# A state-space layer behind attention and experts: the convolution split into even and odd tokens

## Chip, core and metric

One core of one Trainium2 chip runs the whole program. The time is the device time of one execution in microseconds (us). A profile of one further execution gives the rows.

## What is computed

Four layers act on `x` of 8 x 512 tokens by 256 features, in float32, each with a layer norm ahead of it and a residual sum behind it. The third is the one that the change is about:

```
x = x + linear_attention(layernorm(x))        # 16 heads
x = x + one_of_8_experts(layernorm(x))        # 256 -> 512 -> 256, top expert by a router
x = x + ssm(layernorm(x)):
    xc, z = split(x @ in_proj.T)              # 512 and 512 channels
    u  = conv1d(xc, conv_w[512,512,4 taps], causal) + conv_b      # over tokens
    dt = clip(sigmoid(u @ dt_w.T + dt_b), 1e-4, 1);  B, C = u @ B_w.T, u @ C_w.T
    state[t] = exp(clip(dt*A)) * state[t-1] + dt*B*u + 1e-6       # 512 channels x 16 states
    y  = sum over states(state * C) + D*u;  out = (y * silu(z)) @ out_w.T
x = x + one_of_8_experts(layernorm(x))        # the same expert weights again
```

Per output channel the convolution is a sum over 4 taps and 256 features, since the kernel first multiplies the projection and the taps together into one weight `tapw`.

## The kernel before, in words

The program has five parts on one time axis: attention (to some 182 us), a router and the preparation of expert tiles (to 238), 39 expert tiles (to 393), the state-space layer (to 1263), and router and expert tiles once more (to 1469).

The engines are PE (matmul), ACT (activations and copies), DVE (vector), POOL (GpSimd) and SP (issues DMAs). Each runs its own list of instructions in order, and semaphores tie them together.

The state-space layer walks over 8 batches. A batch has 16 states by 4 channel tiles, `SLOTS` = 64 slots. In each slot `g`:

- ACT computes a decay `exp(dt*a)` for slot `g + 3` (`m_decay`, L745) and a quarter of the inputs of the next state (`m_input`, L755).
- PE turns the inputs from tokens-on-partitions to channels-on-partitions with four transposes into one of three banks (`m_spread`, by the helper of L1300).
- DVE runs the recurrence over 512 tokens (`m_scan`, L1197).
- After every four slots POOL multiplies the four results by the row of C (`c_product`, L500) and issues a DMA that adds them to one of two running sums, even or odd states (`add_on`, L509).

Beside the slots of batch `b`, the engines do the preparation of batch `b + 1` (`m_prep` on PE, `m_pre` on ACT and DVE) and the close of batch `b - 1` (`m_close`, `m_late`, `m_skip`). At which slot each of these steps stands is written out by hand in tables of slot numbers: `CONV_AT` for the matmuls of the convolution (L1567), `UT_AT` for the transposes of u (L1575), `BC_AT` (L1584), `DT_AT` (L1598), `DTT_AT` (L1613), `Z_AT` (L1629), `OUT_AT` (L1640), `ADD_AT` for DVE's additions of the two running sums (L1147, L1154), `FINAL_AT` (L1159), `SKIP_AT` for ACT's D*u (L736). `SPIN_AT` are three matmuls without use (L1699). DVE's add of the even sum waits for the last even DMA of the batch before, the semaphore `m_chain0`.

The convolution of one channel tile is 8 matmuls of 512 tokens, 4 taps by 2 halves of the features, summed in one bank; ACT then adds the bias and writes u (`m_uevac`, L699). A float32 matmul stands in the profile as two records, called passes here; a transpose is one record.

Before the first slot stands the preparation of batch 0, with nothing to hide behind: layer norm, 4 x 8 matmuls of the convolution, `dt`, transposes, the first inputs, the turning of batch 1 (`m_turn`). Slots begin at 472.25 us. The weights `tapw` are made by 8 products of `ipw` and `cw` (L1449), four beside the first router, four just before the state-space layer. SP loads `ipw` and `cw` at 203 us, behind the stores of attention's result.

The rows of x lie in a ring of four batches in `x`; SP reloads a batch at state 2. The other half of `x` holds buffers of the scan.

## Time and profile before

| | |
|---|---|
| median of 3 runs | 1475.5 us (1467.76, 1475.5, 1475.68) |
| the profiled execution | 1471.08 us, its span 1469.3 us |
| busy, share of the span | PE 93%, DVE 69%, ACT 64%, POOL 59% |
| granted clock of PE, mean | 0.978 |

The shares are means over five parts with different limits. The busy time of PE is over 93% in every part but attention and the routers, so the shares tell little; the rows by batch, further down, tell more. The two parts with experts (238 to 393 us and 1312 to 1469 us) are not touched.

### The profile page before, as it was taken

What the parts mean: (1) busy time and instruction counts of PE and PEld (TensorE: products, weight loads), DVE (VectorE), ACT (ScalarE), POOL (GpSimd) and SP (SyncE); (2) the same over time, 40 slices, a digit from 0 to 9 for tenths busy, and PEclk for the clock granted to TensorE, in tenths of its full rate; (3) what the DMA queues carried; (4) which work ended last, traced back from release to release, by engine and by line L of the source; (5) the groups of instructions that cost most, each with busy time, mean ns of one, the idle gap of its engine ahead of it and who ended that gap; (6) DMA issues with size and microseconds to landing.
All of it is one profiled execution on the core that took longest, in us unless ns stands there. A gap on an engine that the chain in (4) does not pass through costs nothing.

```text
span 1469.3 us, 22230 instructions
## 1 busy us (share of the span) xinstructions
PE 1366.5 (93%) x7040; PEld 949.6 (65%) x7040; DVE 1011.8 (69%) x1529; ACT 937.7 (64%) x1737; POOL 861.1 (59%) x436
## 2 busy tenths in 40 slices
PE   5899998999998999999999999999999887979997
PEld 2566686999744555565655655655656576569996
...
GB/s 301 85 29 29 19 98 144 211 206 210 153 65 16 118 219 195 179 221 186 201 222 181 205 220 176 218 190 193 223 170 204 230 195 234 79 235 203 208 210 82
DMA packets 108229, 248.39 MB, mean 169 GB/s; under 512 B 19097, under 2 KB 49950, under 8 KB 94048
## 3 DMA queue, kind: packets, MB, share of 16 engines
...
q8 instruction: 55, 0.90, 0.2%
...
## 4 chain that ended last, share of the span: by engine, by line
PE 67%; ACT 16%; DVE 10%; issue 4%; DMA 1%; another core or an unknown queue 1%; SPq 0%; DVEq 0%; ACTq 0%; POOLq 0%; POOL 0%
PE ps L1300 11%; PE ps L1513 9%; PE ps L1504 9%; PE ps L1567 7%; ACT arena L745 7%; PE ps L1598 7%; ACT arena L755 7%; PE ps L1325 4%; PE ps L1640 3%; PE ps L1629 3%; DVE arena L1197 3%; PE ps L1362 2%; PE ps L1584 2%; PE ps L1316 2%; PE ps L1449 1%
## 5 line engine op out<-in xcount | busy, mean ns | idle before, releaser
L500 POOL TENSOR_TENSOR arena<-arena 128x2048 f32<-128x2048 f32 x91 | 425.1, 4684 | 118.6 <-DVE arena L1197 117.4
L1300 PEld LDWEIGHTS ps<-cst,arena 128*128 128x128 f32 x2428 | 295.3, 143 | 280.1 <-issue 187.7
L1197 DVE TENSOR_TENSOR_SCAN arena<-arena,ps 128x512 f32<-128x512 f32 x364 | 431.7, 1209 | 62.3 <-PE ps L1300 58.7
L1300 PE MATMUL ps<-cst,arena 128*128 128x128 f32 x2428 | 365.7, 278 | 51.2 <-ACT arena L755 24.3
L745 ACT ACTIVATE arena<-arena,a_neg 128x512 f32<-128x512 f32 x512 | 365.9, 715 | 43.3 <-DVE arena L1197 29.6
L755 ACT ACTIVATE arena<-arena,m_bt 128x512 f32<-128x512 f32 x512 | 362.9, 709 | 3.8 <-DVE arena L1134 2.2
L1567 PE MATMUL ps<-arena,tapw 128*128 128x512 f32 x512 | 255.1, 600 | 0.7 <-ACT arena L693 0.7
L1197 DVE TENSOR_TENSOR_SCAN x<-arena,ps 128x512 f32<-128x512 f32 x148 | 175.7, 1209 | 21.9 <-PE ps L1300 20.6
L500 POOL TENSOR_TENSOR x<-x,arena 128x2048 f32<-128x2048 f32 x36 | 169.8, 4728 | 14.7 <-DVE x L1197 12.7
L1078 DVE TENSOR_TENSOR arena<-ps,arena 128x256 f32<-128x256 f32 x78 | 33.1, 425 | 205.7 <-PE ps L1513 131.4
L456 POOL DMA_INDIRECT arena<-rows,arena x78 | 75.9, 973 | 158.1 <-DVE arena L1058 134.9
L1504 PEld LDWEIGHTS ps<-arena 128*128 128x128 f32 x1248 | 154.7, 196 | 3.8
L1504 PE MATMUL ps<-arena 128*128 128x128 f32 x1248 | 154.9, 279 | 0.0
L1513 PE MATMUL ps<-arena 128*128 x624 | 147.5, 380 | 3.3 <-ACT arena L644 3.3
L637 ACT ACTIVATE arena<-ps 128x256 f32<-128x256 f32 x78 | 30.0, 385 | 157.8 <-PE ps L1300 156.5
L1598 PE MATMUL ps<-arena,dtw 128*128 128x512 f32 x256 | 128.6, 597 | 0.6 <-ACT arena L699 0.6
L1513 PEld LDWEIGHTS ps<-arena 128*128 128x128 f32 x624 | 112.5, 190 | 16.0 <-issue 3.7
L644 ACT ACTIVATE arena<-ps,b1t 128x128 f32<-128x128 f32 x312 | 89.3, 370 | 43.8 <-issue 29.5
L1567 PEld LDWEIGHTS ps<-arena,tapw 128*128 128x128 f32 x512 | 85.1, 193 | 36.1 <-issue 33.7
L447 POOL TENSOR_TENSOR x<-x,arena 128x1024 f32 (+1 forms) x8 | 18.9, 2358 | 120.0 <-DVE arena L868 114.4
L471 POOL DMA_INDIRECT residual<-arena x39 | 39.4, 1011 | 68.4 <-DVE arena L1085 67.2
L471 POOL DMA_INDIRECT out_x<-arena x39 | 39.3, 1008 | 67.5 <-DVE arena L1085 67.5
...
## 6 DMA issues: line engine op xcount, KB each, us to landing
arena<-arena POOLq DMA_DIRECT2D x52, 1024.0 KB, 8.3
...
arena<-c_rows SPq DMA_DIRECT2D x128, 256.0 KB, 3.7
arena<-x POOLq DMA_DIRECT2D x28, 1024.0 KB, 8.4
x<-arena POOLq DMA_DIRECT2D x24, 1024.0 KB, 8.3
...
```

The lines of the kernel that those rows point to most:

```text
L456: g.indirect_dma_start(out=t_x[j % XB], out_offset=None, in_=xs[r], in_offset=bass.IndirectOffsetOnAxis(ap=idx[:, j:j + 1], axis=0))\
L471: g.indirect_dma_start(out=x_mid if r == 0 else T["out"].rearrange("b s d -> (b s) d"), out_offset=bass.IndirectOffsetOnAxis(ap=idx[:, j:j ...
L500: g.tensor_tensor(h, h, m_c[i % RC].unsqueeze(1).to_broadcast([P, KI, SEQ]), ALU.mult)\
L644: last = a.activation(t_ht[par][:, k, :], ps[4 + par][:, k * P:(k + 1) * P], ACT.Relu, bias=b1t[:, row(e), k:k + 1].rearrange("p a b -> p ...
L745: a.activation(m_a[g % RA], m_dt[b % 2][:, k, :], ACT.Exp, scale=a_neg[:, k, n:n + 1])\
L755: a.activation(m_dbt[i % 2][:, c, :], m_wt[b % 2][:, c, :], ACT.Copy, bias=1e-6, scale=m_bt[b % 2][:, c, n:n + 1]).then_inc(S("m_dbt"), 1)
L1197: v.tensor_tensor_scan(out=h[:, k, :], data0=m_a[g % RA], data1=ps[SCAN_BANK[g % 3]][:, :], initial=0.0, op0=ALU.mult, op1=ALU.add).then_i ...
L1300: return t.transpose(bank, src[:, k * P:(k + 1) * P], ident)
L1504: last = t.matmul(ps[4 + par][:, h * P:(h + 1) * P], t_w1[j % WR][:, k, h * P:(h + 1) * P], t_xt[par][:, k, :], start=(k == 0), stop=(k == ...
L1513: last = t.matmul(ps[6 + par][:, 0:D], t_ht[par][:, k, :], w2[:, row(e), k, :].rearrange("p a h -> p (a h)"), start=(k == 0), stop=(k == K ...
L1567: mm = t.matmul(ps[CONV_BANK[o]][:, :], tapw[:, k, d, o * P:(o + 1) * P], m_xt[n % 2][:, d, k:k + SEQ], start=(i == 0), stop=(i == TAPS * ...
L1598: mm = t.matmul(dt_bank(n, o)[:, :], dtw[:, k, o * P:(o + 1) * P], m_u[n % 2][:, k, :], start=(k == 0), stop=(k == KI - 1))
```

## The change

The convolution is computed in two phases of tokens. For an even token and its odd neighbour the four taps are paired, and three products of half the length take the place of four: (1) the sum of two neighbouring taps times the tokens of one phase, which both outputs use, (2) and (3) single taps times the difference of neighbouring tokens, one for each phase. So a channel tile is 12 matmuls of 256 tokens (one 255) in place of 8 of 512. In batches 1 to 7 this is done for tiles 1, 2 and 3, and tile 0 keeps its 8 matmuls; in batch 0 it is done for all four.

What comes with it: POOL forms the sums of taps once for batch 0 (`sum_first`) and once for all others (`tap_sum`), and two differences of tokens per batch after state 15 (`m_differ`, 128 x 512 elements each, every second token of `m_xt`). ACT moves the shared product with the bias into every second column of u (`m_both`, 256 columns) in place of `m_uevac`; DVE adds the two single-phase products to it (`m_join`, 512 columns, the bank read in alternation from its two halves, the shared product read twice each). The sums and the differences lie in `x`, so the ring of rows shrinks to two places: each batch's rows are loaded for the norm at state 8 and again for the final update at state 2 of the next batch but one, on SP. Two batches of rows for the last router are staged in `tapw`.

All tables of slots are rewritten. The add of the even sum goes from slots (7, 8, 10, 15) to (5, 6, 13, 16), and ACT's third D*u now waits for the first final product. SP loads `ipw` and the first two `cw` at the start of the program; the first product of `tapw` stands between the turns of the first router, and the fourth between its counting matmuls. In the preparation of batch 0 the clips and weights of `dt` stand in another order, two of the four inputs of the first slot are computed by DVE, and the turning of batch 1 begins earlier. Semaphores of the two expert stages are shared, which moves no work.

```diff
+HALF = SEQ // 2
+TURN_OF = ((0, 0), (0, 1), (1, 1), (1, 0))
+PARTS, BOTH_END = 3 * len(TURN_OF), len(TURN_OF) - 1
...
-CONV_AT = ((0, 1, 2, 2, 3, 4, 5, 6), (7, 8, 8, 10, 11, 12, 13, 14), (14, 15, 16, 17, 18, 20, 21, 21), (22, 23, 24, 26, 28, 29, 30, 30))
...
+CONV_AT = ((0, 1, 1, 2, 3, 4, 5, 6), (5, 6, 7, 7, 9, 9, 10, 10, 11, 11, 12, 13), (14, 14, 15, 15, 15, 16, 16, 16, 17, 17, 18, 18), (19, 20, 20, 20, 20, 21, 21, 21, 22, 22, 23, 23))
...
+UC_AT = (8, 10, 17, 21)
...
+ADD_AT = ((5, 6, 13, 16), (11, 12, 15, 17))
+FINAL_AT = (11, 15, 18, 19)
+UPDATE_AT = (31, 52)
+STAT_AT = (33, 37, 62, 63)
+SKIP_AT = (0, 4, 12, 17)
+CLIP_AT = (35, 38, 47, 51)
+WT_AT = (39, 41, 50, 58)
...
+        xd_first = first_h(0)[:, 0:2 * KD * HALF].rearrange("p (s k t) -> p s k t", s=2, k=KD)
+        sum_first = first_h(1).rearrange("p (j k n) -> p j k n", j=2, k=KD)
+        m_xd = x[:, CPB:2 * CPB, :].rearrange("p c d -> p (c d)").rearrange("p (s k t) -> p s k t", s=2, k=KD)
+        tap_sum = x[:, 2 * CPB:4 * CPB, :].rearrange("p c d -> p (c d)").rearrange("p (j k n) -> p j k n", j=2, k=KD)
...
+            def send_tap(k):
+                if k >= 2:
+                    sp.wait_ge(S("tap_mm"), KD * (k - 1))
+                sp.dma_start(cw[k % 2], T["conv"][k].rearrange("(k p) d -> p k d", p=P)).then_inc(S(f"ld_cw{k}"), 16)
+
+            sp.dma_start(ipw, T["ip_x"].rearrange("(k p) d -> p k d", p=P)).then_inc(S("ld_cw0"), 16)
+            send_tap(0)
+            send_tap(1)
...
+                    if n == 2 and b >= 2:
                         sp.wait_ge(S("f1_rows"), 16 * (b - 1))
                         if b > 2:
-                            sp.wait_ge(S("ld_again"), 16 * (b - 2))
-                        sp.dma_start(x[:, kept(new):kept(new) + CPB, :],
-                                     x_mid[new * SEQ:(new + 1) * SEQ].rearrange("(c p) d -> p c d", p=P))\
-                            .then_inc(S("ld_again"), 16)
+                            sp.wait_ge(S("ld_late"), 16 * (b - 2))
+                        sp.dma_start(x[:, 0:CPB, :], x_mid[(b - 1) * SEQ:b * SEQ].rearrange("(c p) d -> p c d", p=P))\
+                            .then_inc(S("ld_late"), 16)
+                    if n == N_LOAD and b < BATCH - 2:
+                        sp.wait_ge(S("m_umm"), conv_done(b + 1, KI - 1))
+                        if b:
+                            sp.wait_ge(S("ld_rows"), 16 * b)
+                        sp.dma_start(x[:, CPB:2 * CPB, :],
+                                     x_mid[(b + 2) * SEQ:(b + 3) * SEQ].rearrange("(c p) d -> p c d", p=P))\
+                            .then_inc(S("ld_rows"), 16)
+                    if n == NS - 2 and b == BATCH - 2:
+                        sp.wait_ge(S("m_umm"), conv_done(BATCH - 1, KI - 1))
+                        sp.wait_ge(S("f1_rows"), 16 * (BATCH - 2))
+                        for k in range(RING, BATCH - 2):
+                            sp.dma_start(staged[k], xs[1][k * SEQ:(k + 1) * SEQ, 0:D].rearrange("(c p) d -> p c d", p=P))\
+                                .then_inc(S("ld_back0"), 16)
+                        sp.wait_ge(S("ld_rows"), 16 * (BATCH - 2))
+                        sp.dma_start(x[:, CPB:2 * CPB, :], x_mid[(BATCH - 1) * SEQ:BATCH * SEQ].rearrange("(c p) d -> p c d", p=P))\
+                            .then_inc(S("ld_rows"), 16)
...
+            def sum_taps(out, j):
+                g.tensor_tensor(out[:, j], tapw[:, TAPS - 1 - 2 * j], tapw[:, TAPS - 2 - 2 * j], ALU.add)\
+                    .then_inc(S("m_zero"), 1)
+
+            g.wait_ge(S("tapw"), 2 * KD)
+            sum_taps(sum_first, 1)
+            g.wait_ge(S("tapw"), TAPS * KD)
+            sum_taps(sum_first, 0)
+
+            def m_differ(n):
+
+                g.wait_ge(S("m_xtc"), KD * (n + 1))
+                for s in range(2):
+                    g.tensor_tensor((m_xd if n else xd_first)[:, s], m_xt[n % 2][:, :, PAD + 1 - 2 * s:PAD + SEQ - 2 * s:2],
+                                    m_xt[n % 2][:, :, PAD:PAD + SEQ - 1:2], ALU.subtract).then_inc(S("m_xd"), 1)
+
+            m_differ(0)
+            g.wait_ge(S("m_stat0"), 2)
+            for j in range(2):
+                sum_taps(tap_sum, j)
+            m_differ(1)
+
...
+                if i % NS == DIFFER_AFTER and i // NS < BATCH - 2:
+                    m_differ(i // NS + 2)
...
-            def m_uevac(n, o):
-                a.wait_ge(S("m_umm"), KI * n + o + 1)
+            def m_uevac(n):
+                a.wait_ge(S("m_umm"), conv_done(n, 0, TAPS * KD - 1))
+                if n >= 2:
+                    a.wait_ge(S("m_y0"), KI * (n - 2) + 1)
+                a.activation(m_u[n % 2][:, 0, :], ps[CONV_BANK[0]][:, :], ACT.Identity, bias=mvec[:, 0, 0:1])\
+                    .then_inc(S("m_u"), 1)
+
+            def m_both(n, o):
+
+                a.wait_ge(S("m_umm"), conv_done(n, o, BOTH_END))
                 if n >= 2:
                     a.wait_ge(S("m_y0"), KI * (n - 2) + o + 1)
-                a.activation(m_u[n % 2][:, o, :], ps[CONV_BANK[o]][:, :], ACT.Identity, bias=mvec[:, 0, o:o + 1])\
-                    .then_inc(S("m_u"), 1)
+                a.activation(m_u[n % 2][:, o, 1::2], both_bank(n)[:, o % 2 * HALF:(o % 2 + 1) * HALF], ACT.Identity,
+                             bias=mvec[:, 0, o:o + 1]).then_inc(S("m_both"), 1)
...
+            def m_join(n, o):
+
+                v.wait_ge(S("m_both"), both_done(n, o))
+                if n and o == 1:
+                    v.wait_ge(S("m_u"), KI * n + 1)
+                v.wait_ge(S("m_umm"), conv_done(n, o))
+                u = m_u[n % 2][:, o, :].rearrange("p (t s) -> p t s", s=2)
+                v.tensor_tensor(u, ps[CONV_BANK[o]][:, :].rearrange("p (s t) -> p t s", s=2),
+                                u[:, :, 1].unsqueeze(2).to_broadcast([P, HALF, 2]), ALU.add).then_inc(S("m_u"), 1)
...
+            for c in range(CPB, NCH // 2):
+                row_stats(c)
+            m_join(0, 0)
+            for c in range(NCH // 2, NCH - 1):
+                row_stats(c)
+            link(row_stats(NCH - 1))
+            m_join(0, 1)
+            layer_norm_scales(CPB, NCH)
+            shifts(CPB, NCH)
+            m_join(0, 2)
+            m_join(0, 3)
+            m_clip(0, 0)
+            m_clip(0, 1)
+            m_btcopy(0)
+            m_weigh(0, 0)
+            m_clip(0, 2)
+            m_weigh(0, 1)
+            m_weigh(0, 2)
+            m_clip(0, 3)
+            m_weigh(0, 3)
+            v.wait_ge(S("m_wt"), KI)
+            v.wait_ge(S("m_btc"), 1)
+            for c in range(CPB // 2, CPB):
+                v.tensor_scalar(m_dbt[0][:, c, :], m_wt[0][:, c, :], m_bt[0][:, c, 0:1], 1e-6, ALU.mult, ALU.add)\
+                    .then_inc(S("m_dbt0"), 1)
...
+            def tap_part(n, c):
+                k, d = n // KD, n % KD
+                if c == 0:
+                    t.wait_ge(S(f"ld_cw{k}"), 16 if k else 32)
+                    if n == 0:
+                        t.wait_ge(S("a_xadd"), BATCH)
+                    if n >= 2:
+                        t.wait_ge(S("tapw"), n - 1)
+                mm = t.matmul(ps[TAP_BANK[n]][:, :], ipw[:, c, d * P:(d + 1) * P], cw[k % 2][:, c, :],
+                              start=(c == 0), stop=(c == KI - 1))
+                if c == KI - 1:
+                    mm.then_inc(S("tap_mm"), 1)
...
-                if o == 0 and i == 0:
-                    t.wait_ge(S("m_xtc"), KD * n + 1)
-                if o == 0 and i == TAPS:
-                    t.wait_ge(S("m_xtc"), KD * n + 2)
+                if n and o == 0:
+                    d, k = i // TAPS, i % TAPS
+                    if k == 0:
+                        t.wait_ge(S("m_xtc"), KD * n + 2 if i == 0 else KD * n + d + 1)
+                    mm = t.matmul(ps[CONV_BANK[0]][:, :], tapw[:, k, d, 0:P], m_xt[n % 2][:, d, k:k + SEQ],
+                                  start=(i == 0), stop=(i == TAPS * KD - 1))
+                    if i == TAPS * KD - 1:
+                        mm.then_inc(S("m_umm"), 1)
+                    return
+                part, (d, j) = i // len(TURN_OF), TURN_OF[i % len(TURN_OF)]
+                first, last = i % len(TURN_OF) == 0, (i + 1) % len(TURN_OF) == 0
+                if o == (1 if n else 0) and i == 0:
+                    t.wait_ge(S("m_zero"), 6 if n else 4)
+                    t.wait_ge(S("m_xtc"), KD * (n + 1))
+                if o == (1 if n else 0) and part and first:
+                    t.wait_ge(S("m_xd"), 2 * n + part)
                 if o == 1 and i == 0 and n >= 2:
                     t.wait_ge(S("m_wt"), KI * n)
-                if o >= 2 and i == 0:
+                if o and i == 0:
+                    t.wait_ge(S("m_both"), both_done(n, o) - 1)
+                if o >= 2 and part == 1 and first:
                     t.wait_ge(S("m_utc"), KI * n + o - 1)
-                d, k = i // TAPS, i % TAPS
-                mm = t.matmul(ps[CONV_BANK[o]][:, :], tapw[:, k, d, o * P:(o + 1) * P], m_xt[n % 2][:, d, k:k + SEQ],
-                              start=(i == 0), stop=(i == TAPS * KD - 1))
-                if i == TAPS * KD - 1:
+                if part == 0:
+                    out, lo = both_bank(n), o % 2 * HALF
+                    w = (tap_sum if n else sum_first)[:, j, d, o * P:(o + 1) * P]
+                    mm = t.matmul(out[:, lo:lo + HALF], w, m_xt[n % 2][:, d, PAD - 2 * j:PAD - 2 * j + SEQ - 1:2],
+                                  start=first, stop=last)
+                else:
+                    out, lo = ps[CONV_BANK[o]], (2 - part) * HALF
+                    w = tapw[:, TAPS - part - 2 * j, d, o * P:(o + 1) * P]
+                    mm = t.matmul(out[:, lo + j:lo + HALF], w, (m_xd if n else xd_first)[:, part - 1, d, 0:HALF - j], start=first, stop=last)
+                if i in (BOTH_END, PARTS - 1):
                     mm.then_inc(S("m_umm"), 1)
...
-            for o in range(1, KI):
-                m_dturn(0, o)
-            for c in range(CPB):
+                if k == 1:
+                    m_dturn(0, 1)
+            m_dturn(0, 2)
+            for c in range(XN):
+                m_turn(1, c)
+            m_dturn(0, 3)
+            for c in range(XN, CPB):
                 m_turn(1, c)
             for b in range(BATCH):
                 for q in range(SLOTS):
```

## Rows read from the trace of the kernel before

**Rows 1.** Busy time in windows, one batch of the scan stage each (columns in the first line)

```profile
core 0: us, PE busy (x) PEld busy (x) DVE busy (x) ACT busy (x) POOL busy (x), PEclk, DMA share, GB/s
472.25:567.64 95.39, 92.24 (x428) 53.85 (x429) 82.01 (x78) 91.68 (x150) 81.03 (x31) 0.98 0.76 168
...
767.17:866.78 99.61, 96.44 (x460) 58.69 (x459) 90.87 (x97) 93.37 (x152) 87.06 (x34) 1.00 0.90 201
...
1165.39:1263.02 97.63, 78.61 (x480) 62.55 (x480) 84.68 (x87) 86.05 (x149) 82.56 (x29) 0.91 0.85 201
```

**Rows 2.** Groups of instructions in the fourth batch, 767.17 to 866.78 us

```profile
L1567 PE MATMUL ps<-arena,tapw 128*128 128x512 f32 x65 | 32.5, 593 | 0.0
...
L1147 DVE TENSOR_TENSOR ps<-ps,arena 128x512 f32<-128x512 f32 x4 | 2.7, 675 | 0.0
...
L699 ACT ACTIVATE arena<-ps,mvec 128x512 f32<-128x512 f32 x4 | 2.7, 667 | 0.0
```

**Rows 3.** What PE waited for in the same batch (total, times, longest)

```profile
PE ps L1300 <- ACT arena L755: 1.6, 2, 0.9
PE ps L1575 <- ACT arena L699: 0.9, 1, 0.9
PE ps L1629 <- DVE arena L1139: 0.6, 1, 0.6
```

**Rows 4.** Chain that ended last, in order of time (start, us, what), tiles and preparation

```profile
204.27 10.97 DMA arena<-in_conv
215.38 5.73 PE ps L1449 x8
...
255.71 1.73 PE ps L1513 x8
...
393.29 13.78 PE ps L1449 x32
410.96 12.96 PE ps L1567 x26
```

**Rows 5.** The same chain just ahead of the first scan

```profile
465.22 1.11 PE ps L1613 x4
...
467.08 2.56 ACT arena L755 x4
...
470.18 2.03 PE ps L1300 x8
```

**Rows 6.** Timeline of POOL in the fourth batch (start, us, what, idle before)

```profile
767.29 0.87 POOL L509 DMA_DIRECT2D arena<-arena  x1 [0.30 <-POOL arena L500]
...
784.19 4.54 POOL L500 TENSOR_TENSOR x<-x,arena 128x2048 f32<-128x2048 f32 x1 [1.24 <-DVE x L1197]
...
861.83 4.87 POOL L500 TENSOR_TENSOR x<-x,arena 128x2048 f32<-128x2048 f32 x1
...
867.65 4.86 POOL L500 TENSOR_TENSOR arena<-arena 128x2048 f32<-128x2048 f32 x1
```

**Rows 7.** DMA issues of the page: POOL's adds (KB each, median us to landing)

```profile
arena<-arena POOLq DMA_DIRECT2D x52, 1024.0 KB, 8.3
```

**Rows 8.** Timeline of DVE at the start of the same batch

```profile
771.16 6.41 DVE L1197 TENSOR_TENSOR_SCAN arena<-arena,ps 128x512 f32<-128x512 f32 x5 [0.56 <-PE ps L1300]
777.49 0.68 DVE L1147 TENSOR_TENSOR ps<-ps,arena 128x512 f32<-128x512 f32 x1
```

**Rows 9.** Groups over the whole span: shapes that bound the new operations

```profile
L637 ACT ACTIVATE arena<-ps 128x256 f32<-128x256 f32 x78 | 30.0, 385 | 157.8 <-PE ps L1300 156.5 <-issue 1.3
...
L447 POOL TENSOR_TENSOR x<-x,arena 128x1024 f32 x7 | 16.5, 2356 | 114.4 <-DVE arena L868 114.4
```

**Rows 10.** Groups from 178 to 245 us: one shape with and without strided access

```profile
L1008 DVE TENSOR_TENSOR arena<-arena 128x256 f32<-128x256 f32 x1 | 0.6, 600 | 0.0
...
L1030 DVE TENSOR_TENSOR arena<-arena 128x256 f32<-128x256 f32 x1 | 0.4, 424 | 0.0
```

**Rows 11.** Timeline of DVE in the router, where PE's count came late

```profile
221.65 0.42 DVE L1016 TENSOR_REDUCE arena<-ps 128x8 f32<-128x256 f32 x1 [3.35 <-PE ps L1464]
```

196 lines of the change are left out of this document (97 added, 99 removed).

## The prediction

> **What bounds the kernel now.** I read first where the time lies, then the scan stage batch by batch, then the waits inside one batch. The stage holds 791 of 1469 us, and batches 1 to 6 each take 99.4 to 99.9 us; the fourth stands for the six [rows 1]. What to see there is that all four engines are nearly full: PE 96.4 of 99.6 us, ACT 93.4, DVE 90.9, POOL 87.1. POOL pauses 0.3 us between a product and the DMA that it issues for it [rows 6], 14 times in a batch, of which the norms fill four: 3.0 us that it can't use, so I count it at 90.1. PE is the fullest, and what it waits for adds up to 3.1 us [rows 3], which is the rest of its batch. So PE bounds a batch today, with the next engine 3 us behind it. In batch 0 it is PE 92.2 and ACT 91.7 of 95.4; in batch 7, which has no convolution to prepare, PE has 19 us to spare and yet the batch takes 97.6 [rows 1]. That row warns: taking 18 us of work from PE brought 2 us.
>
> **The convolution on PE.** A pass of 512 columns costs 13.78 / 32 = 0.431 us, one of 256 columns 1.73 / 8 = 0.216 us [rows 4], with the weight loads in it. The time goes with the columns, so shorter matmuls lose nothing. A tile goes from 16 passes of 0.431 (6.9 us) to 24 of 0.216 (5.2 us): -1.7 us. That is -5.1 us for three tiles in each of 7 batches, and -6.9 us for the four tiles of batch 0. Today's share of the convolution in a batch is 64 passes [rows 2]. The shared product reads every second token. No row of this trace shows a matmul that steps over its moving operand. From below the cost is nothing; from above I take a doubled pass, 8 x 3 x 0.216 = 5.2 us per batch, which would eat the gain. I take nothing, since the nearest rows show passes whose time follows the columns alone. The Trainium skill (SBUF — State Buffer, Door 1: The DMA port swizzle) says that float32 may be stepped by up to four elements at full bandwidth; no run here shows it yet, and my sum would be the same by it.
>
> **ACT.** Three evictions of 512 columns at 0.667 us [rows 2] become three of 256 columns; the like from a bank is 0.385 us [rows 9]. That is -0.28 x 3 = -0.8 us; a penalty for writing every second column could take it back, so between -0.8 and 0. ACT: 92.5. Its third D*u now waits for DVE's first final product (slot 12 after slot 11), and behind it stand the decays. ACT works up to three slots ahead of DVE, so I give it nothing, at most 1 us per batch.
>
> **DVE.** Three joins per batch are new. A contiguous one costs 0.675 us, as the additions of the running sums do [rows 2]. But a join takes its bank elements in alternation from two halves and its shared product every second column. The router has the same shape with and without a strided operand: 256 elements cost 600 ns against 424 [rows 10], 0.69 ns more for each element. With that a join is 0.675 + 0.35 = 1.03 us. I take 1.03: the strided row is nearer. So DVE gets +3.1 us (at least +2.0) and stands at 94.0. The Trainium skill (Vector Engine (DVE) Microarchitecture Reference, 5.2 Measured stream behaviour on trn2) gives 1.73 ns against 1.05 per column when one source hops at every element. The row agrees with that. By it a join would be 1.03 us too, and by a rule without such a cost the batch would be 1 us shorter than in my sum.
>
> **POOL.** Two differences of 512 elements per batch. 1024 elements cost 2.356 us [rows 9], so 1.18 each: +2.4 us, POOL at 92.5. No row of POOL reads every second element, so the upper bound is the row of a whole product, 4.87 us each, +9.7 [rows 6]; the lower is 1.18. I take 1.18. They stand behind the last DMA of a batch; the products of states 0 and 1 of the next are queued behind them, and today POOL waits 1.24 us for DVE at state 2 [rows 6], so half of the 2.4 us is hidden there and the rest falls on later waits of the same kind. The norms move by one state, no change.
>
> **SP and the DMA queues.** One or two loads of 512 KB more per batch over 20 MB: the DMA share of a batch is 0.90 now [rows 1], it goes to some 0.94. No wait on a DMA bounds a batch today. The one that is close: the last even add is issued at 767.29 and takes 8.3 us [rows 6, 7], so it lands at 775.6; DVE's add that needs it starts at 777.49 [rows 8]. The change puts it two scans earlier (2 x 1.13), 775.2. So 0.4 us of waiting, and more by as much as POOL falls behind. I take 0.5, up to 2.
>
> **A batch, summed.** Work per batch after: PE 96.4 - 5.1 = 91.3, ACT 92.5, POOL 92.5, DVE 94.0. The bound passes from PE to DVE. Today the fullest engine lies 3.2 us under the batch time with 3 us to the next; afterwards four engines lie within 3 us, each fed by the others, so I expect no less than the 3.2: 94.0 + 3.2 = 97.2, and with part of the wait for the even sum 97.4. That is -2.2 us for each of six batches, -13.2. The reach: 94.5 if PE's 5.1 us come through in full, 99.6 if the other engines take it all. Batch 0 has 13 us of slack on DVE and POOL has no full batch: PE 87.1, ACT 90.9, so ACT bounds, plus 1.9 to 3.7: 92.7, -2.7 us. Batch 7: nothing is removed, 0 (+-1.5).
>
> **Preparation of batch 0.** All of it is on the path [rows 4, 5]. The convolution runs from 410.96 without a pause worth naming, its first passes at 1.2 GHz (12.96 / 26 = 0.50 us each on average); -6.9 us. Its first tap sum must be ready: the last product of `tapw` ends at 393.29 + 13.78 = 407.1 [rows 4] and its copy costs ACT at most the 0.667 us of an eviction. The other sum has filled POOL until 408.4 or so (an estimate: it can start some 1 us before 407.1, when two taps are long there and the constants of batch 0 let POOL go on), and the last one takes 2.36 more: 410.8, just in time for 410.96 (0 to +1). DVE does its joins between the row statistics; the last one is 1.03 us where ACT's eviction was 0.67: +0.4. Both copies of the turned tokens are now awaited: +0.4. At the end, 465.22 to 472.2 us, stand in a row the last turn of dt, its weights, four inputs on ACT (2.56 us), a norm and the last turns of batch 1 with the first spread (2.03). With two inputs on DVE beside ACT's two -1.3; turning batch 1 earlier -1.2; one turn of dt earlier and overlapped -1.5. Sum -6.9 + 0.4 + 0.4 - 4.0 = -10.1 us, between -6 and -12.
>
> **Router ahead of the expert tiles.** PE waits for the DMA of the taps until 215.38 and then needs 5.73 us for the 8 passes of the first product, 0.72 each where 0.431 is its pace at 2.4 GHz, so partly at 1.2 [rows 4]; DVE waits 3.35 us for the count behind it [rows 11]. With the taps there, the first product goes between the turns: PE's logits come up to 4 x 0.86 = 3.4 us later, but the 3.35 us go; the fourth product between the counts costs 0.86 per count, where PE waits for DVE anyway. I take -1 us (-3.4 to +2). What is late next is DVE's own row of small steps, unchanged.
>
> **The whole sum.** -13.2 - 2.7 + 0 - 10.1 - 1 = -27.0 us. From the profiled execution, 1471.1, that gives 1444.1. It lies 4.4 us under the median of the runs (1475.5), from which the sum gives 1448.5. I forecast the middle, 1446.
>
> **Rivals.** Each is given on the same middle.
> - *PE's gain comes through in full* (7 x 5.1 + 10.1 + 1 = 47 us): 1426. For it speaks that PE is the fullest engine now, with only 3.1 us of waits. Against it: it would leave DVE 0.5 us of slack (94.5 - 94.0), and batch 7.
> - *Another engine takes the batch* (DVE's joins, or POOL): batches 0 to 6 stay as they are, only preparation and router gain, 11 us: 1462. For it: batch 7 with 97.6 us at PE's 78.6.
> - *The change doesn't save on PE*, since stepping over the tokens doubles the shared product's passes: also batch 0's gain shrinks by 16 x 2 x 0.216 = 6.9: 1469.
> - *Slower*: POOL. With a difference at cost d, POOL's work in a batch is 90.1 + 2d. It is the largest of the four from d = 2.0 on, and with the 3.2 us of slack the batch exceeds today's 99.6 from d = 3.2. At d = 4.87 it is 90.1 + 9.7 + 3.2 = 103.0, and POOL's lag delays the even sum, at which DVE stands with the scans behind it, by the 2 us of its bound: 105.0, so 7 x 5.4 - 11 = +27: 1500. For it: no row of POOL shows strided input. Against it: the price is four times that of the contiguous row. The Trainium skill (GPSIMD Engine Reference, 7. Performance pitfalls for Q7 kernels) has a penalty only above 8 bytes of step, and the step here is 8; by it this rival would fall.
>
> **How the numbers follow.** Chances: forecast 0.53, full gain 0.16, another engine 0.21, no saving on PE 0.04, slower 0.06. The range takes in the first three and the bounds of the unknown costs between them: 1424 to 1464. One per cent (15 us) is about what a measurement of this kernel can tell from no change. Faster by over that (under 1461): forecast, full gain and a third of the third case, 0.76; within it 0.17; slower 0.07 with what is left out.
>
> **What would show it.** In the profile after: 88 passes of the convolution per batch in place of 64, the 72 new ones 0.216 us apart; joins of 1.03 us; differences of 1.2 us; batches of 97.4 us with DVE's busy time the highest, about 94; the first scan 10 to 11 us earlier after the last tile; DVE waiting for a DMA at slot 5. The forecast is wrong if the joins cost 0.7 (shorter batches), if POOL falls a state behind at the batch's end, or if the preparation of batch 0 waits for POOL's sums or DVE's statistics.

## The result, and the profile after

The changed kernel takes 1489.5 us in the median of 12 runs (1479.7 to 1506.8), the kernel before 1475.6 (1466.3 to 1478.9). The ratio is 1.0104, with a 95% interval of 1.0082 to 1.0126: about one per cent slower, where 2% faster was forecast. The profiled execution took 1487.8 us, its span 1486.0. Ratios here and below are to runs of the kernel before made beside each kernel, and leave out the executions in a slower state of the chip (one of these 12), so they differ by up to 0.2% from the quotient of the medians.

First, where the time went. The first scan starts at 463.59 us in place of 472.25, so the preparation brought 8.7 us. Batch 0 takes 91.2 us (4.2 less). Batches 1 to 6 take 101.3, 100.8, 104.1, 99.1, 102.6 and 103.0 us, 611.0 in sum where they were 597.8: 13.2 us more, and 13.2 less was forecast. Batch 7 takes 115.1 us, 17.5 more. The tail is 1.1 shorter. Busy time in windows, after, batch 0, the fourth and the last, as in [rows 1]:

```profile
core 0: us, PE busy (x) PEld busy (x) DVE busy (x) ACT busy (x) POOL busy (x), PEclk, DMA share, GB/s
463.59:554.79 91.20, 84.76 (x450) 57.65 (x450) 83.70 (x80) 88.61 (x147) 78.23 (x32) 0.99 0.77 171
756.95:861.07 104.12, 93.93 (x483) 65.34 (x482) 92.16 (x99) 92.19 (x152) 92.64 (x37) 0.97 0.91 204
1165.75:1280.86 115.11, 87.44 (x480) 71.57 (x480) 85.61 (x87) 86.38 (x148) 82.53 (x29) 0.79 0.80 191
```

What to see: in the fourth batch every engine has 10 us or more to spare. No engine bounds it; the engines wait. The last batch has 0.79 of PE's clock where it had 0.91.

The new operations cost what one could hope for. Groups by form, after, fourth batch (against [rows 2, 9]; L1694 is the first tile's convolution, L1715 the shared product of a tile, L1720 its second phase, L1214 the join, L558 POOL's differences):

```profile
L1694 PE MATMUL ps<-arena,tapw 128*128 128x512 f32 x17 | 8.6, 594 | 0.0
L1720 PE MATMUL ps<-x,tapw 128*128 128x256 f32 x24 | 8.0, 420 | 0.0
L1720 PE MATMUL ps<-x,tapw 128*128 128x255 f32 x24 | 7.7, 421 | 0.0
...
L1715 PE MATMUL ps<-arena,x 128*128 128x256 f32 x24 | 6.6, 389 | 0.0
...
L558 POOL TENSOR_TENSOR x<-arena 128x512 f32<-128x512 f32 x2 | 2.4, 1358 | 0.0
...
L1245 DVE TENSOR_TENSOR ps<-ps,arena 128x512 f32<-128x512 f32 x4 | 2.7, 680 | 6.7 <-DMA arena<-arena 6.7
...
L1214 DVE TENSOR_TENSOR arena<-ps,arena 128x512 f32<-128x512 f32 x3 | 2.0, 671 | 0.0
```

The mean ns of a matmul (594) includes its overlap with the next one; the pace, which is shorter, is in the chain below. The one group with idle time ahead of it that stands out is L1245, DVE's addition of the even sum: 6.7 us in this batch, in which DVE waits for a DMA.

Now what DVE and POOL wait for in batches 1 to 6 together, after (total, times, longest):

```profile
POOL arena L582 <- DVE arena L1297: 18.8, 17, 2.3
POOL arena L575 <- DMA c_rows<-arena: 18.7, 5, 5.4
...
DVE ps L1245 <- DMA arena<-arena: 22.5, 4, 6.7
...
DVE ps L1245 <- DMA x<-x: 2.8, 1, 2.8
DVE ps L1245 <- DMA arena<-x: 2.3, 1, 2.3
```

The same view of the kernel before, the largest rows of DVE:

```profile
DVE arena L1197 <- PE ps L1300: 36.4, 75, 1.6
...
DVE x L1197 <- PE ps L1300: 12.7, 26, 1.6
```

Both DMA waits are new: before, DVE waited for the scans' inputs from PE and for no DMA. DVE waits 27.6 us for the even sum, once in every batch. POOL waits 18.7 us at the first norm of a batch (L575) for the store of C (`c_rows<-arena`). Batch by batch the two go together: POOL's wait in batches 0 to 5 is 2.1, 2.2, 5.4, 2.1, 4.6 and 4.4 us, DVE's in batches 1 to 6 is 3.9, 2.8, 6.7, 2.3, 5.7 and 6.1 us. How one leads to the other is seen on POOL's timeline ahead of the fourth batch; the norm stands some 32 us before that batch starts:

```profile
724.53 0.55 POOL L575 TENSOR_SCALAR arena<-x,scales,nw 128x256 f32<-128x256 f32 x1 [5.39 <-DMA c_rows<-arena]
...
758.13 4.56 POOL L582 TENSOR_TENSOR arena<-arena 128x2048 f32<-128x2048 f32 x1 [1.52 <-DMA arena<-c_rows]
762.99 0.87 POOL L591 DMA_DIRECT2D arena<-arena  x1 [0.30 <-POOL arena L582]
```

and on DVE's timeline of that batch:

```profile
759.79 5.12 DVE L1297 TENSOR_TENSOR_SCAN arena<-arena,ps 128x512 f32<-128x512 f32 x4 [0.53 <-PE ps L1423]
771.58 0.70 DVE L1245 TENSOR_TENSOR ps<-ps,arena 128x512 f32<-128x512 f32 x1 [6.67 <-DMA arena<-arena]
```

The batch starts at 756.95. The last even add is issued at 762.99, 6.0 us into it; before it was 0.1 us [rows 6]. DVE asks for the sum at 764.9, 8.0 us into the batch; before it asked 10.3 us into it [rows 8]. So one comes 5.9 us later and the other 2.3 earlier. Right ahead of that add POOL also waits 1.52 us for a row of C (the line at 758.13), so not all of the 5.9 us comes from the norm. DVE waits 6.67 us, and the scans stand behind the addition.

SP's timeline has the store for which POOL waited there, and a load of 512 KB ahead of it, which the change put there:

```profile
706.63 0.64 SPq L457 DMA_DIRECT2D x<-residual  x1
712.68 0.32 SPq L441 DMA_DIRECT2D arena<-c_rows  x1
715.07 0.32 SPq L432 DMA_DIRECT2D c_rows<-arena  x1
```

The store lands at 724.4, 9.4 us after its issue. In batches 0 to 5 it takes 6.0 to 9.4 us, in the seventh batch, which has no load ahead of it, 5.8; in the trace of before it took 3.2 to 4.2. POOL is ready for the norm 4.0 to 5.2 us after the store's issue. Before, the norm began 5.3 to 5.5 us after it, when the store had landed for 1.3 to 2.4 us.

The last batch opens with a longer wait. DVE's timeline there, then what PE and POOL wait for in the whole of it:

```profile
1165.75 3.43 DVE L1297 TENSOR_TENSOR_SCAN arena<-arena,ps 128x512 f32<-128x512 f32 x3
1179.86 3.44 DVE L1297 TENSOR_TENSOR_SCAN arena<-arena,ps 128x512 f32<-128x512 f32 x3 [10.68 <-PE ps L1423]
```

```profile
PE ps L1423 <- DMA tapw<-rows: 10.8, 1, 10.8
...
POOL arena L582 <- DMA arena<-c_rows: 20.3, 3, 13.5
```

PE's 10.8 us are its first turn of the second router's rows, for batch 4. Before, these rows lay in the ring in `x`; now they are staged into `tapw` by a DMA. SP's timeline shows when:

```profile
1149.95 0.37 SPq L393 DMA_DIRECT2D rows<-x  x1
1153.00 0.32 SPq L441 DMA_DIRECT2D arena<-c_rows  x1
1158.52 1.82 SPq L464 DMA_DIRECT2D tapw<-rows  x2
1160.38 1.34 SPq L467 DMA_DIRECT2D x<-residual  x1
1161.77 22.31 SPq L441 DMA_DIRECT2D arena<-c_rows  x3
```

Three transfers of 512 KB are issued one behind the other, and the rows of C for the last batch follow them. SP stands from 1153.0 to 1158.5, since the load of batch 5's rows waits until their own store (issued at 1149.95) has landed.

The preparation of batch 0 is the part that came nearest to the forecast. The chain that ended last, after:

```profile
393.02 13.77 PE ps L1554 x32
411.28 3.75 PE ps L1715 x8
415.04 4.38 PE ps L1720 x16
419.41 1.82 PE ps L1715 x8
...
426.29 1.82 PE ps L1715 x8
...
433.16 1.82 PE ps L1715 x8
```

From the second tile on one starts every 6.9 us, with the turns of u and the products for B and C between; 8 passes of the shared product take 1.82 us, that is 0.228 each, and 0.216 was the price of a contiguous one [rows 4].

### The profile page after: what moved, and what is told of

Its sections match the earlier page's. It is cut to its first block, busy times and chain, and to the rows that moved or that the text cites. A ratio compares the mean times of both kernels' runs of the same rounds, so it can differ in the third digit from the quotient of the medians.

```text
span 1486.0 us, 22746 instructions
## 1 busy us (share of the span) xinstructions
PE 1344.6 (90%) x7240; PEld 1002.4 (67%) x7240; DVE 1025.9 (69%) x1556; ACT 928.8 (63%) x1735; POOL 886.4 (60%) x456
## 3 DMA queue, kind: packets, MB, share of 16 engines
q1 hardware_dynamic: 88752, 119.44, 26.4%
## 4 chain that ended last, share of the span: by engine, by line
PE 57%; issue 11%; POOL 10%; DMA 8%; DVE 8%; ACT 5%; DVEq 0%; POOLq 0%; ACTq 0%
PE ps L1636 9%; PE ps L1645 9%; PE ps L1423 8%; POOL arena L582 5%; PE ps L1748 4%; PE ps L1448 4%; PE ps L1720 3%; DMA arena<-c_rows 3%; DMA arena<-arena 3%; PE ps L1790 2%; PE ps L1485 2%; DVE arena L1297 2%; PE ps L1734 2%; POOL x L582 2%; PE ps L1439 2%
## 5 line engine op out<-in xcount | busy, mean ns | idle before, releaser
L1423 PEld LDWEIGHTS ps<-cst,arena 128*128 128x128 f32 x2428 | 300.8, 146 | 258.5 <-issue 140.1
L582 POOL TENSOR_TENSOR arena<-arena 128x2048 f32<-128x2048 f32 x91 | 431.6, 4759 | 56.2 <-DVE arena L1297 33.3
L1423 PE MATMUL ps<-cst,arena 128*128 128x128 f32 x2428 | 376.2, 283 | 89.7 <-ACT arena L841 36.7
L1297 DVE TENSOR_TENSOR_SCAN x<-arena,ps 128x512 f32<-128x512 f32 x148 | 175.5, 1209 | 14.7 <-PE ps L1423 11.6
L1748 PE MATMUL ps<-arena,dtw 128*128 128x512 f32 x256 | 125.6, 593 | 0.0
L1720 PE MATMUL ps<-x,tapw 128*128 128x256 f32 (+1 forms) x336 | 92.4, 396 | 0.0
L1720 PEld LDWEIGHTS ps<-x,tapw 128*128 128x128 f32 x336 | 61.3, 200 | 6.0
## 6 DMA issues: line engine op xcount, KB each, us to landing
x<-in_x SPq DMA_DIRECT2D x8, 512.0 KB, 11.1
```

The lines of the kernel that those rows point to most:

```text
L582: g.tensor_tensor(h, h, m_c[i % RC].unsqueeze(1).to_broadcast([P, KI, SEQ]), ALU.mult)\
L1297: v.tensor_tensor_scan(out=h[:, k, :], data0=m_a[g % RA], data1=ps[SCAN_BANK[g % 3]][:, :], initial=0.0, op0=ALU.mult, op1=ALU.add).then_i ...
L1423: return t.transpose(bank, src[:, k * P:(k + 1) * P], ident)
L1720: mm = t.matmul(out[:, lo + j:lo + HALF], w, (m_xd if n else xd_first)[:, part - 1, d, 0:HALF - j], start=first, stop=last)
L1748: mm = t.matmul(dt_bank(n, o)[:, :], dtw[:, k, o * P:(o + 1) * P], m_u[n % 2][:, k, :], start=(k == 0), stop=(k == KI - 1))
```

## The experiments

Each is the changed kernel with an edit, unless another one is named. The kernel before ran beside them in each of four groups: 1477.8 us (experiments 1 to 4), 1471.4 (5 to 8), 1472.9 (9 to 12) and 1473.2 (13 to 16). These differ by up to 6.4 us, so kernels of different groups are compared by their distance to the kernel before, or by the ratios. Times of batches are those of one profiled execution each, and that execution is not always a typical one; where it lies far from the median, this is said.

**1. The three loads at the end of the seventh batch, apart.** The store of batch 5's rows is still awaited at state 14.

```
+STAGE_AT = (8, 14, 11)
-if n == NS - 2 and b == BATCH - 2:
-    for k in range(RING, BATCH - 2):          # both staged loads, then the rows
+if b == BATCH - 2 and n in STAGE_AT[0:2]:     # one staged load at state 8, one at 14
...
+if b == BATCH - 2 and n == STAGE_AT[2]:       # the rows of the last batch at state 11
```

> The changed kernel, with the three 512 KB loads that SP issues together at state 14 of the seventh batch (two staged batches and the rows of the last) put at states 8, 11 and 14 of it, one at a time. Theory (the loads, together, hold up the last batch's rows of C and its staged weights on the DMA engines): the last batch goes from 115 us to 98-102 us, the whole from about 1489 to 1474-1477. Rival (the last batch is long because its engines' order of work is worse, not because of DMA): it stays within 2 us of 115, whole 1487-1491.

Measured: 1490.9 us (ratio to before 1.0104, 1.0050 to 1.0158), the last batch 117.7. The theory of the burst fell, in the form that spacing the loads is enough: the two waits that experiments 4 and 5 come to were still there.

**2. The even sum added later.**

```
-ADD_AT = ((5, 6, 13, 16), (11, 12, 15, 17))
+ADD_AT = ((7, 8, 13, 16), (11, 12, 15, 17))
```

> The changed kernel, with DVE's additions of the even sum put back from slots 5 and 6 to slots 7 and 8 of a batch, where the kernel before had them. Theory (DVE stands at slot 5 for the even sum's DMA, 2.3 to 6.7 us per batch): the wait shrinks by up to two scans, batches 1 to 6 become 1 to 2.3 us shorter, the whole 6 to 14 us. Rival (POOL bounds the batch, and DVE's wait only shows it): DVE waits elsewhere, batches change by under 0.5 us, the whole by under 3 us.

Measured: 1484.7 us (1.0060, 1.0024 to 1.0097). Batches 1 to 6 take 593.3 us in sum, 2.9 less per batch, and DVE waits 4.3 us for the even sum in all six, where it was 27.6. POOL's wait for the store of C is still there, 16.4 us: most of it is now covered. But this profiled execution (1470.2 us) is the fastest of the ten and 14.5 us under their median; by the median the edit gives 4.8 us, less than the 6 to 14 expected.

**3. The norm later.**

```
-NORM_AFTER = (8, 10, 11, 12)
+NORM_AFTER = (9, 10, 11, 12)
```

> The changed kernel, with POOL's first norm of a batch put back from behind product 8 to behind product 9, where the kernel before had it. It waits there for the store of C, and POOL's products stand behind it for 2.1 to 5.4 us per batch. Theory (POOL's lag at this wait delays the even sum): POOL's wait falls below 1.5 us, the even sum lands 2 to 3 us earlier, batches 1 to 6 are 1 to 3 us shorter, the whole 6 to 18 us. Rival (the lag comes from the differences alone, 2.35 us per batch): no batch changes by over 0.5 us, the whole by under 3 us.

Measured: 1485.4 us (1.0064, 1.0028 to 1.0100). Batches 1 to 6: 599.2 us, 2.0 less per batch. The wait for the store of C is gone from the list, DVE's for the even sum falls to 18.2 us. The whole is 4.1 us less, where 6 to 18 were expected: in this execution the last batch (118.5 us) and the part behind it (4.3 us longer than in the changed kernel) take back most of the 11.8 us of the six batches.

**4. All three.**

> The changed kernel with all three edits: loads of the seventh batch spread, even sum added at slots 7 and 8, first norm behind product 9. Theory (DMA waits ate the gain, and the work taken from PE is worth something when they are gone): 1445 to 1462 us, the steady batches 97.5 to 99.5 us, clearly below the kernel before. Rival (DVE and POOL, with 2 to 3 us more of work each, take the batch whatever the waits): the steady batches stay at 100 us or more, the whole at 1468 to 1478 us, no better than the kernel before.

Measured: 1469.9 us (0.9950, 0.9920 to 0.9979), which is 19.6 us below the changed kernel and faster than the kernel before. Batches 2 to 6 take 97.9 to 98.1 us. Of the whole this is above the expected range, mainly because the last batch stays at 114.5. PE's wait for `tapw<-rows` is 8.3 us there, with the loads apart. SP's timeline in this run says why:

```profile
1133.21 0.81 SPq L394 DMA_DIRECT2D rows<-x  x1
1141.56 0.32 SPq L442 DMA_DIRECT2D arena<-c_rows  x1
1145.96 0.37 SPq L465 DMA_DIRECT2D tapw<-rows  x1
1147.30 16.00 SPq L442 DMA_DIRECT2D arena<-c_rows  x3
```

The store of batch 5's rows, issued at 1133.21, takes 12.7 us to land; SP stands until then, and asks for the load at 1145.96. The first turn of the last batch waits for both staged loads on one semaphore, so for this late one too, though it needs only the early one.

**5. That wait mended.** Experiment 4, and the load of batch 5's rows behind state 15 with a semaphore of its own; the first turn waits for batch 4's load alone.

```
-STAGE_AT = (8, 14, 11)
+STAGE_AT = (8, 15, 11)
...
-    .then_inc(S("ld_back0"), 16)
+    .then_inc(S("ld_back0" if k == RING else "ld_row5"), 16)
...
-t.wait_ge(S(f"ld_back{b // 2 % 2}"), 64 if b < 2 else 32)
+t.wait_ge(S("ld_row5" if b == RING + 1 else f"ld_back{b // 2 % 2}"), 48 if b < 2 else 32 if b < RING else 16)
```

> The kernel with all three edits, and beside them: the staged rows of the sixth batch are asked for after state 15 of the seventh batch, where their own store has landed, in place of state 14, and have a semaphore of their own, so that the first turn of the last batch doesn't wait for them. Theory (SP's queue stands at state 14 for that store, 1133.2 to 1145.9 us in the run with all three, and the rows of C of the last batch are queued behind it; spreading the loads alone could not help): the last batch goes from 114.5 to 99-104 us, the whole from 1470 to 1455-1461. Rival (the last batch is long for its own order of work): over 111 us, the whole 1466-1474.

Measured: 1462.9 us (0.9957, 0.9925 to 0.9989). That is 7 us under experiment 4, but the kernel before, run beside it, was 6.4 us faster too, and the ratios (0.9950 there) are the same: on the whole no gain is shown. The last batch takes 111.1 us: the stall of its first slots is gone (its first four slots 4.9 us in place of 12.8), but at slot 7 DVE waits 3.8 us for the sum `x<-arena`, which lands 16.6 us into the batch where before it was 8.1. The expectation of 99 to 104 us for the batch and 1455 to 1461 for the whole missed.

**6. The same in the changed kernel, without the two edits of the steady batch.**

> The changed kernel with the loads spread and the staged rows of the sixth batch asked for after state 15 with their own semaphore, nothing else. Theory (SP's wait at state 14): the last batch 99-104 us, the whole 1474-1479 (1489 less 11 to 15). Rival (own order of work): 113-117 us, the whole 1486-1492.

Measured: 1488.5 us (1.0116, 1.0082 to 1.0150); last batch 109.0. By the batch the theory gains, by the whole nothing is seen: the six batches ahead of it were longer in that execution (614.9 us, 611.0 in the changed kernel).

**7. PE's work given back.** Experiment 5, and two matmuls of 512 columns ahead of the second phase of each tile.

```
+if n and part == 1 and first:
+    for _ in range(2):
+        t.matmul(out[:, :], ones, cst[:, 0:4 * P], start=True, stop=True)
```

> The kernel of the run with the last batch mended, with the work that the change took from PE given back: two matmuls of 512 columns (four passes, 1.72 us) ahead of the second phase of each of the three tiles, 5.2 us per batch in seven batches; the outputs are not changed by them. Theory (PE bounded the batch before, and what the change takes from it is worth something): the steady batches go from 98.0 to 101-103 us, the whole 20 to 35 us longer. Rival (the batch is set by the row of dependent steps between ACT, PE and DVE, or by DVE with 92 us, and not by PE's work): the steady batches 98.0 to 99.0, the whole less than 7 us longer.

Measured: 1479.0 us (1.0061, 1.0027 to 1.0094), 16.1 more than experiment 5. PE's busy time goes from 91.7 to 96.4 us in a batch; the steady batches go from about 98 to 100.1 (one 101.3), batch 0 from 91.2 to 95.6. Busy time in windows of a steady batch, of this run:

```profile
860.70:960.81 100.11, 96.35 (x496) 65.82 (x494) 92.68 (x100) 93.06 (x153) 90.44 (x38) 1.00 0.92 208
```

It is the batch of the kernel before (99.6 with PE 96.4 [rows 1]) but for half a microsecond. Between the two expectations: of 5.2 us given back, 1.9 per steady batch count (11.4 in six) and 4.4 in batch 0. So what the change takes from PE is worth something, and not all of it.

**8. No differences on POOL.** Experiment 5 without L558 in batches 0 to 5, and PE's wait for the differences lowered to match.

```
+if n >= 2:
+    return
```

> The kernel of the run with the last batch mended, without POOL's two differences in batches 0 to 5 (for batches 2 to 7 the second phase of the convolution reads what lies there, so the outputs are other ones). Theory (once the even sum is added late enough, POOL's 2.35 us per batch lie beside other work): the steady batches stay within 0.4 us of 98.0, the whole within 4 us. Rival (POOL's lag still bounds them): the steady batches fall by 1 to 2.3 us, the whole by 6 to 14 us.

Measured: 1462.1 us (0.9935, 0.9902 to 0.9969), 0.8 less than experiment 5; batches 2 to 6 take 97.9 to 98.9 us, as there. POOL's added work costs nothing that can be seen once the waits are mended. The last batch, in which nothing was changed, takes 113.6 us here and 109.1 in experiment 7, for 111.1 in experiment 5: so much one profiled batch scatters.

**9. The load in front of the store of C, one state earlier.** `N_LOAD = 7` for 8.

> The changed kernel with the 512 KB load of the rows of the batch after next asked for after state 7 in place of state 8, so one more row of C lies between it and the store of C (after state 9) on SP's queue. Theory (the load right ahead of the store is what makes the store land late, 9 us and more, and POOL's first norm wait for it): POOL's wait at the norm falls by 1 to 3 us in each of batches 0 to 5, batches 1 to 6 are 0.5 to 2 us shorter, the whole 4 to 12 us. Rival (the store is late whatever stands ahead of it, since all queues are full): within 3 us of the changed kernel.

Measured: 1493.0 us (1.0140, 1.0077 to 1.0203). POOL's wait for the store of C falls from 18.7 to 10.2 us, but not because the store lands earlier: it still takes 6.3 to 9.5 us. POOL comes to the norm later, 5.0 to 7.1 us after the store's issue in batches 1 to 5, where it was 4.0 to 4.1, since it now waits 10.4 us for rows of C (2.0 in the changed kernel). The wait has moved. DVE waits 28.3 us for the even sum as before and the six batches take 611.7; the time is that of the rival.

**10. The rows of the last batch loaded in that batch.** Experiment 5 with this, and the second of the four staged loads of the last batch one state later.

```
-if b == BATCH - 2 and n == STAGE_AT[2]:
+if b == BATCH - 1 and n == STAGE_AT[2]:       # STAGE_AT = (8, 15, 8)
...
-BACK_AT = (1, 2, 5, 6)
+BACK_AT = (1, 3, 5, 6)
```

> The kernel with the last batch mended (111.05 us for that batch), with one 512 KB load more taken out of its beginning: the rows of the last batch are loaded again after state 8 of that batch itself, and the second of the four staged loads after state 3 in place of 2. Theory (rows of C land in 9 to 11 us where 512 KB transfers stand beside them, POOL falls behind by 4 us at the end of the seventh batch, and the last even sum lands 16.6 us into the last batch where before it was 8.1): POOL catches up by 2 to 4 us, the last batch takes 104-108 us, the whole 3 to 7 us less than 1462.9. Rival (the clock of PE, at 0.5 for most of the first half of the last batch, sets its length): 110-112 us.

Measured: 1459.0 us (0.9918, 0.9887 to 0.9949), the fastest of the study with experiments 11 and 13. The interval overlaps that of experiment 5, and two edits were made at once. Busy time in windows, a steady batch and the last:

```profile
753.00:850.93 97.93, 91.64 (x484) 63.37 (x482) 92.16 (x99) 92.65 (x153) 90.39 (x37) 1.00 0.94 212
1144.80:1251.99 107.19, 91.17 (x480) 74.80 (x480) 85.20 (x87) 86.96 (x148) 83.38 (x30) 0.78 0.85 202
```

DVE's list of waits in batches 1 to 6 of this run, now without a wait for the even sum:

```profile
DVE arena L1300 <- PE ps L1426: 17.7, 37, 0.8
DVE x L1300 <- PE ps L1426: 7.5, 14, 0.9
DVE arena L1300 <- ACT arena L834: 3.1, 4, 0.8
DVE x L1300 <- ACT arena L834: 1.6, 2, 0.8
DVE x L1300 <- DMA arena<-arena: 0.5, 1, 0.5
```

**11. PE kept busy in the last batch.** Experiment 10, and a matmul of 256 columns into an unused bank at each of the first 32 slots of the last batch.

> The same as the kernel with the rows in the last batch, and beside it one matmul of 256 columns (0.43 us at 2.4 GHz) into an unused bank at each of the first 32 slots of the last batch, 13.8 us of work more on PE; the outputs are not changed by it. Theory of the clock (PE idles while it waits for transfers, is granted 1.2 GHz behind it, and then its spreads set the pace: 0.62 to 0.73 mean clock over the first half, 0.74 to 0.90 before the change): the clock stays above 0.9 and the last batch is 4 to 10 us shorter than without these matmuls. Rival (the transfers alone set the length): the clock goes up and the batch stays within 2 us, or is longer by the added work.

Measured: 1459.5 us (0.9918, 0.9889 to 0.9947). The last batch of the profiled execution:

```profile
1143.18:1243.73 100.55, 88.30 (x545) 71.74 (x543) 85.22 (x87) 86.31 (x148) 83.59 (x29) 0.93 0.91 218
```

The clock goes from 0.78 to 0.93, the batch from 107.2 to 100.6 us. But the median of the whole doesn't move; the profiled execution (1452.6 us) is the fastest of the ten.

**12. The early addition alone, in the kernel before.** `ADD_AT` (5, 6, 10, 15) for (7, 8, 10, 15) there.

> The kernel before the change, with one part of the change alone: DVE adds the even sum at slots 5 and 6 in place of 7 and 8. There the even sum lands 8.3 to 9.7 us into the batch. Theory (the early addition costs a wait as soon as POOL isn't ahead): DVE waits 0.5 to 2 us per batch at slot 5 and the steady batches are 0 to 1 us longer, the whole 0 to 7 us longer. Rival (the early addition alone is the whole loss of the steady batches, 2 to 3 us each): the whole 12 to 20 us longer.

Measured: 1479.4 us against 1472.9 (1.0047, 1.0017 to 1.0078); the profiled execution took 1472.2. DVE waits 7.1 us for the even sum in six batches, and these take 603.5 us, 1.0 more each:

```profile
DVE ps L1147 <- DMA arena<-arena: 3.8, 4, 1.4
DVE ps L1147 <- DMA x<-x: 1.9, 1, 1.9
DVE ps L1147 <- DMA arena<-x: 1.4, 1, 1.4
```

**13. Experiment 11 with 44 slots in place of 32.**

> The kernel with all waits mended and matmuls of 256 columns into an unused bank in the first 44 slots of the last batch (32 in the run before, where the profiled last batch was 100.6 us against 107.2 without them while the medians of the whole, 1459.5 and 1459.0, showed no gain). Theory of the clock (its gain is real, and the medians were covered by the scatter of some 10 us): clock of the last batch at or above 0.9, the batch 99 to 102 us, the whole 3 to 7 us below 1459. Rival (the length of the last batch varies by several us from one execution to the next whatever the clock): the whole within 3 us of 1459.

Measured: 1459.7 us (0.9916, 0.9883 to 0.9949). Clock 0.93, last batch 104.3. Within 3 us of 1459: the gain of the clock is not shown. In both runs the part behind the last scan is some 2 us longer (207.1 and 206.9 against 205.0), which takes part of it.

**14 and 15. One edit of experiment 10 taken back: the addition at slots 5 and 6, or the norm behind product 8.**

> The kernel with all waits mended (1459.0 us, steady batches 97.94), with the even sum added at slots 5 and 6 again, as the change has it. Theory (both edits of the steady batch are needed, since each wait alone lets POOL fall behind the even sum): the steady batches go to 98.8-100.2, DVE waiting for the sum's DMA at slot 5 in most of them, the whole 6 to 14 us longer. Rival (the norm was the cause and the addition only showed it): steady batches below 98.4, the whole less than 4 us longer.

> The kernel with all waits mended (1459.0 us, steady batches 97.94), with POOL's first norm behind product 8 again, as the change has it. Theory: POOL waits 2 to 5 us per batch for the store of C, the steady batches go to 98.3-99.5, the whole 3 to 9 us longer. Rival (with the even sum at slot 7 POOL's wait is covered): steady batches below 98.3, the whole less than 3 us longer.

Measured: 1466.0 us (0.9966, 0.9942 to 0.9991) and 1466.5 (0.9958, 0.9933 to 0.9984). With the early addition the batches 1 to 6 take 97.6 to 101.1, DVE waiting 15.2 us for the sum. With the early norm POOL waits 16.3 us for the store of C, and a batch takes either 97.9 to 98.0 us (behind waits of 2.2 to 2.8 us at the norm) or 100.3 to 100.5 (behind 4.4 to 5.5), three of each.

**16. Experiment 10 without the two edits of the steady batch.**

> The changed kernel with the loads about its last batch placed as in the best kernel (staged batch at state 8, the other after state 15 with its own semaphore, the rows of the last batch in that batch, the second staged load of it at state 3), and the two edits of the steady batch left out. Theory (the last batch's own loads and SP's wait made it 115 us; what POOL lags there adds some): the last batch 105-110 us, the whole 5 to 12 us below 1489. Rival (the last batch is long mainly because POOL arrives late in it, from the even sum and the norm): 111-115 us, the whole within 4 us of 1489.

Measured: 1484.4 us (1.0092, 1.0064 to 1.0120), 5 below the changed kernel. Its profiled execution took 1502.7 us, 18 above the median, so only the time is used.

The four kernels with the loads of the last batch placed in the same way make a square, and medians stand in it:

| | norm behind product 8 | norm behind product 9 |
|---|---|---|
| even sum at slots 5, 6 | 1484.4 | 1466.0 |
| even sum at slots 7, 8 | 1466.5 | 1459.0 |

Here either edit alone brings 18 us, the other then 7. The profiled batches 1 to 6 say the same in both arrangements of the last loads: 608 to 615 us in sum with neither edit (the changed kernel, experiments 1, 6 and 9), 593.3 and 594.9 with the later addition alone, 599.2 and 596.4 with the later norm alone, 588.0 to 591.2 with both. They are two ends of one chain: the norm makes POOL late, and the early addition makes DVE wait for POOL's last DMA. With neither edit, POOL is late and DVE asks early.

The medians of experiments 2 and 3 do not agree with the square. In the changed kernel with its own last loads, the same edits alone brought only 4.8 and 4.1 us, and both with the loads spread 19.6. What an edit is worth on the whole thus hangs on how the last loads are placed; why so much is not shown.

One profiled last batch scatters by some us, but over all kernels (without experiment 16) it follows the arrangement of its loads: 113.5 to 118.5 us in the six that experiment 5 had not yet mended (the changed kernel, experiments 1 to 4 and 9), 109.0 to 113.6 in experiments 5 to 8, 105.5 to 109.3 in the three that load the last rows in that batch (10, 14, 15), and 100.6 and 104.3 with PE kept busy besides (11, 13).

## Why the prediction was wrong

From the forecast to the measurement is 43.7 us by the profiled executions (-27.0 forecast, +16.7 measured). Batches 1 to 6 make 26.4 of them (-13.2 forecast, +13.2 measured), the last batch 17.5, preparation and router 2.4; batch 0 and the tail are 2.6 better.

The convolution on PE, and the cost of the added instructions, were right or better. The stepped shared product runs at 1.82 / 8 = 0.228 us a pass in batch 0, against 0.216 taken; PE's work in a steady batch is 91.6 us, 91.3 forecast. So the rival "no saving on PE" is out. A difference costs 2.35 / 2 = 1.18 us, as taken, and experiment 8 shows that the two cost nothing by themselves: the price at which the rival "slower" was to begin, d = 3.2, never came. A join costs 0.671 us and not 1.03. That was the price on the row of the router [rows 10], which read every second element of SBUF; a bank's two halves taken in alternation had no such cost. The Trainium skill's rate for a source that hops at every element (Vector Engine (DVE) Microarchitecture Reference, 5.2 Measured stream behaviour on trn2), by which a join would be 1.03 us too, was measured on a tile in SBUF, and this read shows that it doesn't carry over to a bank. ACT's term was mis-sized in the other direction: the evictions with a bias were priced by one without (0.385 us), and take 0.482, so three of them give 0.6 us and not 0.8.

The preparation was nearly right: the first scan came 8.7 us earlier, for -11.1 forecast with the router. The router's -1 did not come (the last tap product starts at 393.02, before at 393.29). Batch 0 gave 4.2 for 2.7.

"A batch, summed" said 97.4 us, and with the waits mended the steady batch is 97.9. That this is so near is luck. Two terms were off and cancel: the fullest engine is ACT with 92.7 (DVE has 92.2, not 94.0), and the batch lies 5.3 us above it, not 3.2. Experiment 7 shows that some of that distance is PE's as well: with 4.7 us more on PE the batch is some 2 us longer.

What failed stands under three other words.

First, "SP and the DMA queues". The margin was seen, 0.4 us of waiting at the early addition, "and more by as much as POOL falls behind", with an end at 2. In the kernel before, that edit alone costs 1.0 us per batch (experiment 12), inside this. In the changed kernel DVE waited 2.3 to 6.7 us, because POOL fell behind by up to 5.9 us. The amount by which POOL falls behind had been left out of the bound.

Second, "The norms move by one state, no change" under POOL. This is the step that failed. The norm waits for the store of C (L575 behind `m_cst`), and I moved it one state earlier while the store moved one state earlier too, and took the two for a pair. The store's landing was not in the sum: it takes 6.0 to 9.4 us where it took 3.2 to 4.2, and so it lands after POOL has come to the norm. Of the 26.4 us of the six batches, 11.8 go with the norm one product later (experiment 3), and 20 to 23 when the addition comes two slots later as well (experiments 4, 5 and 10). That makes 5 waits, 18.7 us, on the engine whose lag I had named as the danger. Experiments 3 and 15 show the wait and its price: 7.5 us on the whole where all else is mended. Why the store lands later is open. The load of 512 KB ahead of it was my theory; with the load one state earlier (experiment 9) the store still took 6.3 to 9.5, and the whole did not gain. The seventh batch speaks for a part of it: its store took 5.8 to 6.4 us in the four kernels that put no load ahead of it (the changed kernel, experiments 2, 3 and 9), and 6.2 to 12.9 in those that do (experiments 1, 4 to 8, 10, 11, 13 to 15; most near 8). Even the former is above the 3.2 to 4.2 of before, so the load is not the whole reason.

Third, "Batch 7: nothing is removed, 0 (+-1.5)". Nothing is removed, but what was kept in the ring must be loaded again, and I counted the loads of a steady batch (DMA share 0.94, measured 0.93 to 0.94 in the mended kernels) and not those that gather at the end: three of 512 KB at state 14 of the seventh batch. My first theory, that they crowd the queues together, fell in experiment 1. What held its first slots up was two waits, SP's for the store behind state 14 and the first turn's for both loads: with both mended, the first four slots take 4.9 us in experiment 5, where they took 15.2 in the changed kernel, 12.8 in experiment 4 and 4.5 before. The batch gains less, 114.5 to 111.1 us, since later slots wait in turn, and on the whole the gain doesn't show. With the rows of the last batch out of the way it takes 107.2 (experiment 10). The whole, 3.9 us less, is again within its interval. Some 10 us of the 17 remain. PE has its clock at 0.78 there, where it was 0.91, and with it at 0.93 the profiled batch took 100.6 and 104.3 us (experiments 11 and 13), for 105.5 to 109.3 without, yet the medians did not follow. Whether the clock is a cause of those 10 us or goes with them is open.

The rival that came nearest, "slower", had the right chain (POOL's lag, the even sum, DVE standing with the scans behind it) and the wrong trigger: it made the lag hang on the price of a difference, when it came from a wait. Of the signs that the prediction named for being wrong, two came: joins of 0.7 us, and POOL nearly a state behind at the batch's end (5.9 us; a state is 6.2).
